# Expert results kept in slot order and gathered back by token half, and rotated sums moved to VectorE

## The chip, the cores and the metric

The kernel runs on one core of a Trainium2 chip. The metric is the device time of one execution in microseconds; of several runs the median stands.

## The reference

The input is x, 4 x 1024 tokens of width 256, float32. One block of the Macaron kind: half a feed-forward layer, attention, half a feed-forward layer, each behind a layer norm. The feed-forward layer sends every token to two of eight experts (width 176).

```python
def _L0_ffn_ref(hidden_states, gate_w, w_gate, w_up, w_down):
    x = hidden_states.reshape(-1, d)
    probs = jax.nn.softmax((x @ gate_w.T).astype(jnp.float32), axis=-1)
    top_w, sel = jax.lax.top_k(probs, TOP_K)                  # TOP_K = 2 of E = 8
    top_w = top_w / jnp.sum(top_w, axis=-1, keepdims=True)
    w_te = jnp.zeros((t, e), logits.dtype).at[jnp.arange(t)[:, None], sel].add(top_w)
    g = jnp.einsum('td,edf->tef', x, w_gate)
    u = jnp.einsum('td,edf->tef', x, w_up)
    out = jnp.einsum('tef,efd->td', silu(g) * u * w_te[:, :, None], w_down)

def _L0_attn_ref(hidden_states, Wq, Wk, Wv, Wo):              # 16 heads of 16
    q, k, v = (proj(Wq), proj(Wk), proj(Wv))
    # _apply_rope: concatenate([x1 * cos - x2 * sin, x2 * cos + x1 * sin])
    q, k = _apply_rope(q, cos, sin), _apply_rope(k, cos, sin)
    probs = softmax(q k^T / 4 + causal)
    return (probs v) Wo^T

x = x + 0.5 * _L0_ffn_ref(_layernorm(x), ...)
x = x + _L0_attn_ref(_layernorm(x), ...)
x = x + 0.5 * _L0_ffn_ref(_layernorm(x), ...)
```

## The kernel before

**Tiles and phases.** The 4096 tokens are 32 token tiles of 128 rows; x_sb holds them in SBUF all the time. Phases run one after the other, with a barrier between: set-up, ffn_phase (f1), projection_phase, attention_phase, output_phase, ffn_phase (f2). Every engine has its own program, written out in order; semaphores connect them. There is no scheduler: what stands first in an engine's program is done first, and an instruction that waits holds up all behind it on its engine.

**Routing in ffn_phase.** Normalised rows go to xn_dram. VectorE picks each token's two experts, and ranks turn into a slot number for each of the 8192 pairs (token, choice). The pairs of one expert lie in a row of slot tiles of 128; with every expert's last tile filled up there are at most SLOT_TILES = 71 of them. Which token stands in which slot is found by one-hot products: VectorE compares slot_p with all rows (at_row, L493) and slot_j with all slot tiles (tile_hits, L475 to L477), in four lots of 16 columns of pairs, and TensorE multiplies the two (64 matmuls over the first 16 slot tiles; 64 of 110 columns over the other 55, L670). `owners` (L483 to L486) makes of the products the row to which each slot's result goes (pair_i) and the token that it reads (token_i). Then comes the list of the experts by tile (L510 to L520), on which TensorE's first expert product waits.

**Expert steps.** For each slot tile j: POOL gathers 128 rows of xn_dram by token_i with an indirect DMA (L378, seventeen steps ahead); TensorE turns it, multiplies by the gate and up weights (L691), turns h (L699) and multiplies by the down weights (L709), each in high and low parts; ScalarE and VectorE do what lies between, ScalarE's last piece being y_copy (L593) into y_sb, eight tiles deep. Two steps later POOL scatters the tile to y_dram by pair_i with a second indirect DMA (L382). So y_dram holds the results by token: both rows of a token side by side. SP has nothing to do in these steps; it waits for the last scatter.

**The end of f2.** SP loads y_dram, 256 KB a token tile (L362), VectorE adds both weighted rows to x_sb (L554), ScalarE issues eight output stores of 512 KB.

**Projection.** f1's results are added here. SP loads y in the same 256 KB pieces (L938, eight deep); ScalarE weighs the first row (L1065), POOL adds it (mix_first, L976), VectorE weighs and adds the second (mix_second, L1038), eight tiles ahead of the projection. VectorE's moments (L112 and those behind it) go into the norm factors, once for four tiles, on POOL (L981, L982). Then for each token tile: ScalarE normalises, TensorE turns and projects q, k and v, VectorE multiplies q and k by cosines and sines (turn_angles: L1023, L1026, L1027), POOL adds the two products (add, L993, roped), TensorE turns the sum, and it is split in three parts by ScalarE, VectorE (rest, L1032), ScalarE and POOL (r_low, L987), and stored by SP. At step t an engine works on tile t, or on t−2 and t−3 where it comes later in this chain.

## Time and profile before

| | us |
|---|---|
| Median of three runs | 1216.24 |
| The runs' span | 1216.02 to 1219.74 |
| The profiled execution | 1216.84 |
| Its span in the trace | 1215.1 |
| Expert steps of f1, 99.36 to 266.68 | 167.32 |
| Projection, 275.39 to 409.34 | 133.95 |
| Expert steps of f2, 1004.75 to 1173.32 | 168.57 |
| Behind f2's last y_copy, 1173.32 to 1215.10 | 41.78 |

Over the span TensorE is busy for 83%, VectorE for 70%, ScalarE for 52% and POOL for 48%; such shares are means over stages with different limits. Stages are read one at a time: the windows say which engine is full in a stage, the chain of waits which engine was last at a place, the timelines when an instruction began, how long it took, and in brackets how long its engine had been idle before it and what ended that. A busy POOL during an indirect DMA is the time in which it makes the transfer's list, not the transfer.

### The profile page before, as it was taken

What the parts mean: (1) busy time and instruction counts of PE and PEld (TensorE: products, weight loads), DVE (VectorE), ACT (ScalarE), POOL (GpSimd) and SP (SyncE); (2) the same over time, 40 slices, a digit from 0 to 9 for tenths busy, and PEclk for the clock granted to TensorE, in tenths of its full rate; (3) what the DMA queues carried; (4) which work ended last, traced back from release to release, by engine and by line L of the source; (5) the groups of instructions that cost most, each with busy time, mean ns of one, the idle gap of its engine ahead of it and who ended that gap; (6) DMA issues with size and microseconds to landing.
All of it is one profiled execution on the core that took longest, in us unless ns stands there. A gap on an engine that the chain in (4) does not pass through costs nothing. (4 is left out here: it accounts for less than half of the span.)

```text
span 1215.1 us, 24056 instructions
## 1 busy us (share of the span) xinstructions
PE 1002.9 (83%) x6998; PEld 644.2 (53%) x6998; DVE 846.8 (70%) x2632; ACT 630.8 (52%) x1318; POOL 588.9 (48%) x756
## 2 busy tenths in 40 slices
PE   1649998974888489999999999999988569998850
PEld 1438997863767223333333333333347349998750
DVE  5585444435999498999989998988529684443347
ACT  1504554444777216666666666666774505554430
POOL 2937777765999302222222222222239127777740
PEclk9857999996999659999999999999989858999985
DMA  6803333325565511111111111110022413333349
GB/s 212 278 12 102 105 102 104 105 92 158 155 180 164 161 61 47 57 56 60 59 57 57 56 60 55 55 54 2 2 75 71 140 31 105 104 103 104 104 149 338
DMA packets 84524, 121.19 MB, mean 100 GB/s; under 512 B 10920, under 2 KB 63920, under 8 KB 81200
## 3 DMA queue, kind: packets, MB, share of 16 engines
q1 hardware_dynamic: 63424, 75.08, 19.8%
q0 software_dynamic: 13632, 37.24, 9.7%
q10 hardware_dynamic: 7344, 7.34, 1.8%
q8 instruction: 63, 1.03, 0.4%
q14 instruction: 61, 0.50, 0.1%
HBM read 75.51 MB, written 43.78 MB: 98 GB/s over the span
## 5 line engine op out<-in xcount | busy, mean ns | idle before, releaser
L1352 ACT ACTIVATE a_probs<-a_ps_s 128x1024 f32<-128x1024 f32 (+3 forms) x384 | 294.2, 813 | 172.8 <-PE a_ps_s L1384 171.6
L1267 POOL TENSOR_SCALAR_AFFINE_SELECT a_probs<-a_probs 128x256 f32<-128x256 f32 x256 | 102.9, 408 | 368.9 <-ACT a_probs L1352 366.2
L1285 DVE CUSTOM_DVE_ANT_0 a_unused<-a_ps_m,const_sb 128x128 bf16<-128x128 f32 (+3 forms) x512 | 234.1, 485 | 26.6 <-PE a_ps_m L1369 16.7
L1369 PE MATMUL a_ps_m<-st_k,st_q 96*128 96x512 bf16 (+3 forms) x768 | 219.6, 344 | 22.3 <-PEq L167 14.9
L378 POOL DMA_INDIRECT v_sb<-xn_dram,f_token_i x142 | 139.7, 984 | 104.7 <-DVE f_token_i L486 62.0
L1287 DVE TENSOR_REDUCE a_max_a<-a_ps_m 128x1 f32<-128x512 f32 x256 | 175.7, 686 | 13.9 <-PE a_ps_m L1369 13.7
L1384 PE MATMUL a_ps_s<-st_q,st_k 98*128 98x512 bf16 (+3 forms) x768 | 180.6, 329 | 1.5 <-ACT a_probs L1352 1.4
L532 DVE TENSOR_TENSOR f_h<-f_ps_gu,f_sg 128x176 f32<-128x176 f32 x142 | 48.5, 341 | 185.2 <-ACT f_sg L598 185.1
L1369 PEld LDWEIGHTS a_ps_m<-st_k,st_q 96*128 96x128 bf16 x768 | 67.8, 98 | 194.3 <-DVE a_max_a L1287 55.2
L1397 PE MATMUL a_ps_ctx<-a_probs,a_v_st 128*32 128x512 f32 (+3 forms) x1536 | 163.6, 498 | 1.3 <-POOL a_probs L1267 0.7
L382 POOL DMA_INDIRECT y_dram<-v_sb,f_pair_i x142 | 140.0, 986 | 44.0 <-issue 38.1
L593 ACT ACTIVATE v_sb<-f_ps_y 128x256 f32<-128x256 f32 x142 | 54.7, 385 | 109.3 <-DMA y_dram<-v_sb,f_pair_i 82.1
L1384 PEld LDWEIGHTS a_ps_s<-st_q,st_k 98*128 98x128 bf16 x768 | 65.3, 98 | 72.3 <-ACT a_probs L1352 42.6
L691 PE MATMUL f_ps_gu<-w_gu_hi,f_xT_hi 128*128 x284 | 96.1, 338 | 9.1 <-DVE f_xT_lo L527 4.2
L691 PE MATMUL f_ps_gu<-w_gu_hi,f_xT_lo 128*128 x284 | 93.2, 328 | 0.0
L691 PE MATMUL f_ps_gu<-w_gu_lo,f_xT_hi 128*128 x284 | 93.0, 327 | 0.0
L709 PE MATMUL f_ps_y<-w_dn_hi,f_hT_hi 88*128 x284 | 92.5, 326 | 0.1
L709 PE MATMUL f_ps_y<-w_dn_lo,f_hT_hi 88*128 x284 | 80.1, 282 | 0.0
L709 PE MATMUL f_ps_y<-w_dn_hi,f_hT_lo 88*128 x284 | 79.4, 280 | 0.0
L588 ACT ACTIVATE f_xT_hi<-f_ps_xT 128x256 fp32r<-128x256 f32 x142 | 54.0, 380 | 46.9 <-PE f_ps_xT L681 46.5
L598 ACT ACTIVATE f_sg<-f_ps_gu 128x176 f32<-128x176 f32 x142 | 44.8, 316 | 53.4 <-PE f_ps_gu L691 53.4
L699 PE MATMUL f_ps_hT<-const_sb,f_h 128*88 128x128 f32 x284 | 55.7, 278 | 10.3 <-DVE f_h L532 9.9
(193 smaller groups left out, 2018.8 us busy)
## 6 DMA issues: line engine op xcount, KB each, us to landing
xn_dram<-v_sb SPq DMA_DIRECT2D x64, 128.0 KB, 3.7
v_sb<-y_dram SPq DMA_DIRECT2D x32, 256.0 KB, 5.5
st_q<-qk_dram SPq DMA_DIRECT2D x16, 384.0 KB
st_k<-qk_dram SPq DMA_DIRECT2D x16, 384.0 KB
st_q<-y_dram SPq DMA_DIRECT2D x16, 256.0 KB, 3.3
st_k<-y_dram SPq DMA_DIRECT2D x16, 256.0 KB, 3.2
qk_dram<-st_rT_hi SPq DMA_DIRECT2D x16, 256.0 KB, 3.0
qk_dram<-st_rT_mid SPq DMA_DIRECT2D x16, 256.0 KB, 3.5
```

The lines of the kernel that those rows point to most:

```text
L378: pool.indirect_dma_start(xg[:, slot, :], None, xn_dram, bass.IndirectOffsetOnAxis(ap=token, axis=0)).then_inc(gathered[slot], 16)
L382: pool.indirect_dma_start(y_dram, bass.IndirectOffsetOnAxis(ap=pair, axis=0), y_sb[:, slot, :], None).then_inc(scattered[slot], 16)
L691: mm = pe.matmul(ps_gu[b][:, 0:2 * F], x_part[:, b, k, :], w_part[:, bass.ds(e, 1), k, :].rearrange("p a f -> p (a f)"), start=(n == 1), s ...
L699: mm = pe.transpose(ps_hT[b][:, c, :], h[:, b, c * FH:(c + 1) * FH], ident)
L709: mm = pe.matmul(ps_y[b], h_part[:, b, c, :], w_part[:, bass.ds(e, 1), c, :].rearrange("p a f -> p (a f)"), start=(n == 1), stop=(n == 6))
L1267: pool.affine_select(out=tri, in_=tri, compare_op=ALU.is_ge, fill=zero, base=0, pattern=[[0, 2], [1, P]], channel_multiplier=-1).then_inc( ...
L1285: dve.tensor_tensor_reduce(unused[:, bank, 0:nk], ps, cst("mask")[:, HALF - nk:HALF], 1.0, NEG, ALU.add, ALU.max, at).then_inc(taken, 1)
L1287: dve.tensor_reduce(at, ps, AX.X, ALU.max).then_inc(taken, 1)
L1352: act.activation(probs[:, s % 4, :, 0:nq], ps_s[s % 2][:, :, 0:nq], ACT.Exp, scale=float(HD) ** -0.5).then_inc(exp_done, 1)
L1369: pe.matmul(ps_m[bank][:, 0:nk], q_st[b][0:MAX_ROW, h, P * i:P * i + P], k_st[b][0:MAX_ROW, h, k0:k0 + nk], start=True, stop=True).then_in ...
L1384: mm = pe.matmul(ps_s[s % 2][:, n, 0:nq], k_st[b][:, h, P * j:P * j + P], q_st[b][:, h, q0:q0 + nq], start=True, stop=True)
L1397: mm = pe.matmul(ps_ctx[32 * h:32 * h + 32, q0 - HALF * half:HALF], v_st[b % 2][:, j, h, :], probs[:, (2 * v + h // 2) % 4, h % 2, 0:nq], ...
```

## The change

**Slots by token half.** The pairs of the first 16 token tiles get the slot tiles 0 to 38, those of the other 16 the tiles 39 to 77: each half with its own list of experts and its own filling, 78 tiles in place of 71. The weights are indexed by tile, as before. The one-hot products run in three passes: slot tiles 0 to 15 and 16 to 38 over the first half's two lots, 39 to 77 over the second half's two, with 32 matmuls each. `owners` no longer makes pair_i.

**Results in slot order.** SP stores each y tile as it stands (plain DMA, 128 KB, L383). The slot number of each pair stays in SBUF as y_rows, and a row group of 128 results is gathered back from y_dram by an indirect DMA on POOL (gather_y). There are 64 such groups, two for each token tile.

**First half's rows.** In both passes its 32 groups are gathered inside the expert loop, one a step from step 43 on, behind one wait for the first 39 stores, and added to x_sb by VectorE from step 46 on. In f2 SP also stores the first four outputs inside the loop.

**Second half's rows.** In f2 POOL waits for all stores and gathers the 32 groups one after the other; VectorE adds them, ScalarE stores. In f1 they are gathered in the projection, five in four steps from step −7 to step 17 (GATHERS), weighed by ScalarE two steps later, and added by POOL another step later; VectorE no longer adds a row there.

**Rotated sums.** `add` (the sum that goes into roped) is issued by VectorE, behind `rest`, in place of POOL.

Cut to its core:

```diff
-SLOT_TILES = TOPK * NT + E - 1
+HALVES = 2
+HT = NT // HALVES
+CT = TOPK * HT + E - 1
+SLOT_TILES = HALVES * CT
+ROWS_OF_HALF = TOPK * HT
 LOT = 16
 LOTS = TOPK * NT // LOT
 DEEP = 8
 XDEEP = 16
+YB = 8
+Y_LAG = 4
+MIX_LAG = 3
...
+def token_row(m):
+
+    return 2 * (m // 4) + m % 2, m // 2 % 2
+
+def rows_mixed(t):
+
+    return 4 * (t // 2) + t % 2 + 3
...
+        LOTS_OF = [range(half, LOTS, HALVES) for half in range(HALVES)]
+        PASSES = [(0, FIRST, LOTS_OF[0]), (FIRST, CT, LOTS_OF[0]), (CT, SLOT_TILES, LOTS_OF[1])]
+        at_tile = [sb(f"at_tile{i}", [P, len(lots), 2 * (j1 - j0), LOT], BF16) for i, (j0, j1, lots) in enumerate(PASSES)]
...
+        OUT_AT = [CT + Y_LAG + MIX_LAG + 8 * (q + 1) - 1 for q in range(HT // 4 - 1)] + [SLOT_TILES - 1]
+
+        def store_out(eng, q):
+
+            eng.wait_ge(mixed, 8 * (q + 1))
+            eng.dma_start(out[q * 4 * P:(q + 1) * 4 * P, :].rearrange("(t p) d -> p t d", p=P), x_sb[:, 4 * q:4 * q + 4, :]).then_inc(out_stored, 16)
...
+            for j in range(SLOT_TILES):
+                sp.wait_ge(y_out, j + 1)
+                sp.dma_start(y_dram[j * P:(j + 1) * P, :], y_sb[:, j % DEEP, :]).then_inc(stored[j % DEEP], 16)
+                if out is not None and j in OUT_AT:
+                    store_out(sp, OUT_AT.index(j))
             for q in range(DEEP):
-                sp.wait_ge(scattered[q], 16 * len(range(q, SLOT_TILES, DEEP)))
+                sp.wait_ge(stored[q], 16 * len(range(q, SLOT_TILES, DEEP)))
             if out is not None:
-                for t in range(NT):
-                    sp.wait_ge(mixed, t - 7 + 8)
-                    sp.dma_start(yb[:, t % 8, :, :].rearrange("p c d -> p (c d)"),
-                                 y_dram[t * P * TOPK:(t + 1) * P * TOPK, :].rearrange("(p c) d -> p (c d)", c=TOPK)
-                                 ).then_inc(y_in[t % 8], 16)
                 sp.wait_ge(out_stored, 16 * (NT // 4))
...
-            def scatter(j, slot, pair):
-                pool.wait_ge(y_out, j + 1)
-                pool.indirect_dma_start(y_dram, bass.IndirectOffsetOnAxis(ap=pair, axis=0), y_sb[:, slot, :], None).then_inc(scattered[slot], 16)
-
-            def step(j, u, token, pair):
-
-                if token is not None:
-                    if j + XDEEP + 1 == FIRST:
-                        pool.wait_ge(slots_ready, 2)
+            def gather_y(m):
+                t, c = token_row(m)
+                wait(pool, mixed, m - YB + 1)
+                row = y_rows[:, c * NT + t:c * NT + t + 1]
+                pool.indirect_dma_start(yg[:, m % YB, :], None, y_dram[0:CT * P, :] if m < ROWS_OF_HALF else y_dram, bass.IndirectOffsetOnAxis(ap=row, axis=0)).then_inc(y_in[m % YB], 16)
+
+            def wait_stored(tiles):
+                for q in range(DEEP):
+                    pool.wait_ge(stored[q], 16 * len(range(q, tiles, DEEP)))
+
+            for j in range(-XDEEP - 1, SLOT_TILES + 2):
+                ahead = j + XDEEP + 1
+                if is_tile(ahead):
+                    if ahead in (FIRST, CT):
+                        pool.wait_ge(slots_ready, 2 if ahead == FIRST else 3)
                     wait(pool, xT_ready, j + 2)
-                    gather((j + XDEEP + 1) % XDEEP, token)
-                if pair is not None:
-                    scatter(j - 2, (j - 2) % DEEP, pair)
-
-            def fixed_step(j):
-                step(j, j % 4, token_i[:, j + XDEEP + 1:j + XDEEP + 2] if is_tile(j + XDEEP + 1) else None, pair_i[:, j - 2:j - 1] if is_tile(j - 2) else None)
-
-            for j in range(-XDEEP - 1, SLOT_TILES + 2):
-                fixed_step(j)
+                    gather(ahead % XDEEP, token_i[:, ahead:ahead + 1])
+                if j == CT + Y_LAG:
+                    wait_stored(CT)
+                if 0 <= j - CT - Y_LAG < ROWS_OF_HALF:
+                    gather_y(j - CT - Y_LAG)
+            if out is not None:
+                wait_stored(SLOT_TILES)
+                for m in range(ROWS_OF_HALF, TOPK * NT):
+                    gather_y(m)
...
+            def mix(m):
+                t, c = token_row(m)
+                dve.wait_ge(y_in[m % YB], 16 * (m // YB + 1))
+                if c:
+                    dve.wait_ge(mixed, m - 1)
+                dve.scalar_tensor_tensor(x_sb[:, t, :], yg[:, m % YB, :], w_mix[:, c, t:t + 1], x_sb[:, t, :], ALU.mult, ALU.add).then_inc(mixed, 1)
...
+                if 0 <= j - CT - Y_LAG - MIX_LAG < ROWS_OF_HALF:
+                    mix(j - CT - Y_LAG - MIX_LAG)
...
-            for i in range(TOPK * NT):
-                lot = i // LOT
-                pe.wait_ge(first_hot_ready, lot + 1)
-                mm = pe.matmul(ps_first, at_row[:, lot, :, i % LOT], at_first[:, lot, :, i % LOT], start=(i == 0), stop=(i == TOPK * NT - 1))
-            mm.then_inc(first_owned, 1)
-            for i in range(TOPK * NT):
-                lot = i // LOT
-                pe.wait_ge(later_hot_ready, lot + 1)
-                mm = pe.matmul(ps_later, at_row[:, lot, :, i % LOT], at_later[:, lot % 2, :, i % LOT], start=(i == 0), stop=(i == TOPK * NT - 1))
-                if i % LOT == LOT - 1:
-                    mm.then_inc(later_hot_used if i < TOPK * NT - 1 else later_owned, 1)
+            pe.matmul(ps_before, before_bf[:], hot_sum[:], start=True, stop=True)
+            pe.matmul(ps_total, ones_bf[:, 0:P], hot_sum[:], start=True, stop=True).then_inc(ranks_ready, 1)
+
+            done = 0
+            for i, (j0, j1, lots) in enumerate(PASSES):
+                for n, lot in enumerate(lots):
+                    done = done + 1
+                    pe.wait_ge(one_hot_ready, done)
+                    for k in range(LOT):
+                        mm = pe.matmul(ps_owner[i], at_row[:, lot, :, k], at_tile[i][:, n, :, k],
+                                       start=(n == 0 and k == 0), stop=(n == len(lots) - 1 and k == LOT - 1))
+                mm.then_inc(owned, 1)
...
+GATHERS = {t: [n for n in range(ROWS_OF_HALF) if 4 * n // 5 - 7 == t] for t in range(-20, NT + 20)}
...
+            def gather_y(n):
+                t, c = later_row(n)
+                wait(pool, mixed, n - YB + 1)
+                row = y_rows[:, c * NT + t:c * NT + t + 1]
+                pool.indirect_dma_start(yb(n), None, y_dram, bass.IndirectOffsetOnAxis(ap=row, axis=0)).then_inc(y_in[n % YB], 16)
+
+            def mix(n):
+                t, c = later_row(n)
+                pool.wait_ge(weighted, n + 1)
+                if c:
+                    pool.wait_ge(mixed, n - 1)
+                pool.tensor_tensor(x_sb[:, t, :], yb(n), x_sb[:, t, :], ALU.add).then_inc(mixed, 1)
...
-                if is_tile(t + AHEAD + 1):
-                    mix_first(t + AHEAD + 1)
-                if is_tile(t):
-                    add(t, u % 2)
+                for n in GATHERS[t]:
+                    gather_y(n)
+                for n in GATHERS[t - 3]:
+                    mix(n)
...
+            def add(t, b):
+                dve.wait_ge(angled, 3 * t + 3)
+                wait(dve, rT_ready, t - 1)
+                dve.tensor_tensor(roped[:, b, :].rearrange("p (a j h) -> p a h j", j=HD, h=HG),
+                                  by_cos[:, b, :].rearrange("p (a h j) -> p a h j", j=HD, h=HG),
+                                  by_sin[:, b, :].rearrange("p (a h j) -> p a h j", j=HD, h=HG), ALU.add).then_inc(roped_ready, 1)
...
-            def mix_second(t):
-                dve.wait_ge(begun, t + 1)
-                dve.scalar_tensor_tensor(x_sb[:, t, :], yb(t)[:, 1, :], w_mix[:, 1, t:t + 1], x_sb[:, t, :],
-                                         ALU.mult, ALU.add).then_inc(mixed, 1)
 
             def step(t, u):
                 if t >= 0 and is_tile(t + 1):
                     x_low(t + 1, (u + 1) % 2)
                 if is_tile(t):
                     turn_angles(t, u % 2)
-                if is_tile(t + AHEAD):
-                    mix_second(t + AHEAD)
                 if is_tile(t - 2):
                     rest(t - 2, t - 2)
+                if is_tile(t):
+                    add(t, u % 2)
                 if is_tile(t + AHEAD - 1):
-                    dve.wait_ge(mixed, t + AHEAD)
+                    if t + AHEAD - 1 >= HT:
+                        dve.wait_ge(mixed, rows_mixed(t + AHEAD - 1 - HT))
                     moments_of.tile(t + AHEAD - 1, (t + AHEAD - 1) % 8)
...
+                for n in GATHERS[t - 2]:
+                    weigh(n)
```

POOL from the last expert steps of f1 into the projection, before (the tile named v_sb holds the gathered x and y_sb, st_q and st_k hold y in the projection):

```order
L378 DMA v_sb<-xn_dram,f_token_i 128x256
L382 DMA y_dram<-v_sb,f_pair_i 17280x256 x20
L211 UNCONDITIONAL_BRANCH
L166 ISA x2
L968 UNCONDITIONAL_BRANCH
L971 MEMSET p_minus_half 128x4
L844 MEMSET st_one 32x128
L976 TENSOR_TENSOR x_sb<-st_q,x_sb 128x256 x4
L976 TENSOR_TENSOR x_sb<-st_k,x_sb 128x256 x2
L981 TENSOR_TENSOR rstd<-rstd,p_minus_half 128x4
L982 TENSOR_TENSOR nmr<-nmr,rstd 128x4
```

The same place after:

```order
L402 DMA v_sb<-xn_dram,f_token_i 128x256
L408 DMA v_sb<-y_dram,y_rows 128x256 x15
L227 UNCONDITIONAL_BRANCH
L182 ISA x2
L1001 UNCONDITIONAL_BRANCH
L1004 MEMSET p_minus_half 128x4
L881 MEMSET st_one 32x128
L1011 DMA st_q<-y_dram,y_rows 128x256 x5
L1018 TENSOR_TENSOR x_sb<-st_q,x_sb 128x256 x2
L1023 TENSOR_TENSOR rstd<-rstd,p_minus_half 128x4
L1024 TENSOR_TENSOR nmr<-nmr,rstd 128x4
```

The loop's last POOL work is gathers of y in place of scatters (ahead of these rows they take turns with the gathers of x, one and one, as the scatters did from step 2 on), and in the projection five gathers and two additions stand ahead of the first norm factors, where six additions stood. f2 ends with 47 of L408 in a row.

POOL in the projection, before, from one set of norm factors on:

```order
L981 TENSOR_TENSOR rstd<-rstd,p_minus_half 128x4
L982 TENSOR_TENSOR nmr<-nmr,rstd 128x4
L976 TENSOR_TENSOR x_sb<-st_k,x_sb 128x256
L993 TENSOR_TENSOR p_roped<-p_by_cos,p_by_sin 128x8x4x16
L987 TENSOR_TENSOR st_rT_lo<-p_rT_rest,st_rT_mid 128x4x128
```

The same place after:

```order
L1023 TENSOR_TENSOR rstd<-rstd,p_minus_half 128x4
L1024 TENSOR_TENSOR nmr<-nmr,rstd 128x4
L1011 DMA st_q<-y_dram,y_rows 128x256 x2
L1018 TENSOR_TENSOR x_sb<-st_q,x_sb 128x256
L1029 TENSOR_TENSOR st_rT_lo<-p_rT_rest,st_rT_mid 128x4x128
```

The sum L993 has left POOL, and two gathers have come (one in each of the next three steps).

VectorE in one tile of the projection, before:

```order
L1014 TENSOR_TENSOR p_xT_lo<-p_ps_xT,p_xT_hi 128x256
L1023 TENSOR_TENSOR p_by_cos<-p_ps_qk,const_sb 128x512
L1026 TENSOR_TENSOR p_by_sin<-p_ps_qk,const_sb 128x32x8
L1027 TENSOR_TENSOR p_by_sin<-p_ps_qk,const_sb 128x32x8
L1038 SCALAR_TENSOR_TENSOR x_sb<-st_k,w_mix,x_sb 128x256
L1032 TENSOR_TENSOR p_rT_rest<-p_ps_rT,st_rT_hi 128x512
L112 BN_STATS p_stats<-x_sb 128x6
```

The same tile after:

```order
L1048 TENSOR_TENSOR p_xT_lo<-p_ps_xT,p_xT_hi 128x256
L1056 TENSOR_TENSOR p_by_cos<-p_ps_qk,const_sb 128x512
L1059 TENSOR_TENSOR p_by_sin<-p_ps_qk,const_sb 128x32x8
L1060 TENSOR_TENSOR p_by_sin<-p_ps_qk,const_sb 128x32x8
L1072 TENSOR_TENSOR p_rT_rest<-p_ps_rT,st_rT_hi 128x512
L1065 TENSOR_TENSOR p_roped<-p_by_cos,p_by_sin 128x8x4x16
L128 BN_STATS p_stats<-x_sb 128x6
```

The second mix L1038 has gone, and the rotated sum stands behind the residual.

## Rows read from the trace of the kernel before

**Rows 1.** Windows by stage: stretch, length, busy PE, PEld, DVE, ACT, POOL, clock, DMA.

```profile
99.36:266.68 167.32, 158.45 (x1132) 149.55 (x1132) 72.85 (x212) 86.51 (x283) 127.40 (x132) 0.98 0.33 104
275.39:409.34 133.95, 98.72 (x576) 82.88 (x576) 112.67 (x272) 86.52 (x192) 114.34 (x114) 0.89 0.58 169
1004.75:1173.32 168.57, 158.52 (x1132) 149.32 (x1132) 72.81 (x212) 86.12 (x283) 127.90 (x132) 0.98 0.33 104
1173.32:1215.10 41.78, 0.00 (x0) 0.00 (x0) 27.19 (x64) 0.00 (x0) 1.24 (x2) 0.51 0.86 308
```

**Rows 2.** The chain that ended last, second expert stage: start, us, what.

```profile
1012.17 0.95 PE f_ps_gu L691 x6
...
1073.93 1.10 PE f_ps_gu L691 x6
1075.58 0.97 POOL v_sb L378
...
1078.15 0.97 POOL v_sb L378
...
1173.89 2.42 DMA y_dram<-v_sb,f_pair_i
```

**Rows 3.** Timeline of VectorE, routing of the first pass: start, us, what.

```profile
74.66 1.22 DVE L493 TENSOR_TENSOR v_sb<-f_count_lot,f_slot_p 128x2048 bf16<-128x2048 bf16 x1
...
76.64 1.22 DVE L493 TENSOR_TENSOR v_sb<-f_count_lot,f_slot_p 128x2048 bf16<-128x2048 bf16 x1
...
82.59 0.61 DVE L475 TENSOR_TENSOR f_at_later<-f_count_lot,f_slot_j 128x880 bf16<-128x880 bf16 x1
...
84.25 0.17 DVE L483 SCALAR_TENSOR_TENSOR f_empty<-f_ps_hT,const_sb 128x16 f32<-128x16 f32 x1
...
92.90 0.74 DVE L510 TENSOR_TENSOR f_work<-const_sb,f_first_tile 128x568 f32<-128x568 f32 x1
...
96.37 0.17 DVE L520 CAST f_packed<-f_packed_f 128x10 int32<-128x10 f32 x1
```

**Rows 4.** Timeline of TensorE, the long one-hot product of the first pass.

```profile
84.39 13.39 PE L670 MATMUL f_ps_y<-f_at_later,v_sb 128*128 128x110 bf16 x64 [0.43 <-DVE f_at_later L477]
```

**Rows 5.** Timeline of POOL: gathers of the first pass, first factors of the projection.

```profile
92.97 1.49 POOL L378 DMA_INDIRECT v_sb<-xn_dram,f_token_i  x1 [0.30 <-issue]
...
103.53 0.94 POOL L378 DMA_INDIRECT v_sb<-xn_dram,f_token_i  x1 [0.31 <-issue]
...
285.93 1.22 POOL L981 TENSOR_TENSOR rstd<-rstd,p_minus_half 128x4 f32<-128x4 f32 x1 [1.38 <-DVE nmr L123]
```

**Rows 6.** Windows of the projection, columns as in group 1: four tiles, then three.

```profile
354.82:369.44 14.62, 12.31 (x72) 10.06 (x72) 13.88 (x36) 9.20 (x22) 14.28 (x15) 1.00 0.52 150
388.35:396.62 8.27, 8.27 (x56) 7.48 (x55) 7.00 (x17) 6.31 (x15) 7.32 (x8) 1.00 0.55 164
```

**Rows 7.** Groups by line and shape: xcount, busy us, mean ns, idle before.

```profile
L993 POOL TENSOR_TENSOR p_roped<-p_by_cos,p_by_sin 128x512 f32<-128x512 f32 x32 | 46.0, 1437 | 9.2 <-DVE p_by_sin L1027 8.8
...
L987 POOL TENSOR_TENSOR st_rT_lo<-p_rT_rest,st_rT_mid 128x512 bf16<-128x512 f32 x32 | 37.2, 1163 | 2.4 <-ACT st_rT_mid L1090 2.3
...
L1023 DVE TENSOR_TENSOR p_by_cos<-p_ps_qk,const_sb 128x512 f32<-128x512 f32 x32 | 21.7, 678 | 5.1 <-PE p_ps_v L1129 4.6 <-POOL p_roped L993 0.5
...
L1038 DVE SCALAR_TENSOR_TENSOR x_sb<-st_k,w_mix,x_sb 128x256 f32<-128x256 f32 x16 | 12.1, 759 | 1.6 <-POOL x_sb L976 1.6
L976 POOL TENSOR_TENSOR x_sb<-st_q,x_sb 128x256 f32<-128x256 f32 x16 | 12.1, 763 | 4.1 <-ACT st_q L1065 4.1
...
L981 POOL TENSOR_TENSOR rstd<-rstd,p_minus_half 128x4 f32<-128x4 f32 x8 | 8.3, 1044 | 2.6 <-DVE nmr L123 2.6
...
L438 DVE TENSOR_TENSOR f_hot<-const_sb,f_chosen 128x256 f32<-128x256 f32 x4 | 2.4, 590 | 0.1
```

**Rows 8.** Timeline of VectorE, the last mixes of the kernel.

```profile
1207.25 3.10 DVE L554 SCALAR_TENSOR_TENSOR x_sb<-v_sb,w_mix,x_sb 128x256 f32<-128x256 f32 x7 [0.18 <-DMA v_sb<-y_dram]
```

**Rows 9.** The page's DMA issues: count, KB each, median us to landing.

```profile
xn_dram<-v_sb SPq DMA_DIRECT2D x64, 128.0 KB, 3.7
```

More of the change, by code:

```diff
@@ L440, in _ @@
             dve.wait_ge(lg_ready, NT // 4)
             choose(0, ps_lg)
-            own.then_wait(dve.scalar_tensor_tensor(others[:], hot[:, 0, :, :].rearrange("p e t -> p t e"), NEG, ps_lg, ALU.mult, ALU.add))
+            for half in range(HALVES):
+                of = slice(HT * half, HT * (half + 1))
+                own.inc(dve.scalar_tensor_tensor(others[:, of, :], hot[:, 0, half, :, :].rearrange("p e t -> p t e"), NEG, ps_lg[:, of, :],
+                                                 ALU.mult, ALU.add))
@@ L500, in _ @@
+            for lot in LOTS_OF[0]:
+                row_hits(lot)
+                tile_hits(0, lot)
+            for lot in LOTS_OF[0]:
+                tile_hits(1, lot)
+            owners(0)
+            for lot in LOTS_OF[1]:
+                row_hits(lot)
+                tile_hits(2, lot)
             dve.wait_ge(egap_ready, 1)
@@ L619, in _ @@
             if out is not None:
[L620 to L623 removed]
+                for q in range(HT // 4, NT // 4):
+                    store_out(act, q)
         @block.tensor
@@ L960, in step @@
                     load_stacks((t - 14) // 2)
-            for t in range(YB - 2):
-                load_y(t)
             tiles(sp, step)
```

238 lines of the change are left out of this document (103 added, 135 removed).

## The prediction

> **What bounds the kernel now.** I read the times and the page, then the windows by stage, then the chain that ended last and the timelines where stages meet. The profiled execution took 1216.84 us (span 1215.1), 0.60 above the median of 1216.24, so the sum is made against 1216.84 and 0.60 comes off at the end. In both expert stages TensorE is busy for 158 of some 168 us at a clock of 0.98 [rows 1]. POOL is at 127: each step it issues a gather and a scatter, two indirect DMAs, and in the chain they stand 2.57 us apart (1075.58 to 1078.15) where the products of an expert step go on every 2.13 us (1012.17 to 1073.93, 29 tiles) [rows 2]. So POOL falls behind, and the chain runs through it in the stage's second part. In the projection VectorE and POOL are both nearly full: of a stretch of four tiles, 14.62 us, they are busy for 13.88 and 14.28; late, when no y is left to mix, a tile takes 2.76 us (8.27 over three) and TensorE is full, VectorE busy 7.00 [rows 6]. After the last product of the second pass nothing runs on TensorE for 41.78 us: y comes back and is mixed there [rows 1].
>
> **Routing, twice.** From the first one-hot operation (74.66) to the first expert product (99.36) are 24.70 us [rows 1, 3]. TensorE's second one-hot product sets the end: 64 matmuls of 110 columns, 13.39 us, 0.21 each [rows 4], and VectorE is through with its list at 96.54 [rows 3]. Now 96 matmuls run in place of 128, none wider than 78 columns, over half the lots each. VectorE's work: two lots of 16 tiles as before, 1.98 each (74.66 to 76.64); two lots of 23 tiles, below the 1.66 that a lot of 55 takes (82.59 to 84.25), I take 1.1; owners, three operations of some 0.2, twice 0.6; two lots of 39 tiles with their rows, 1.22 for the rows and below 1.66 for the tiles, I take 2.6; the weights of the mix 0.9 (estimate: four operations of 0.17 to 0.35 with gaps); the expert list as before, 3.64 (92.90 to 96.54) [rows 3]. Together 4.0 + 2.2 + 1.2 + 5.2 + 0.9 + 3.6 = 17.1. TensorE's last 16 matmuls start when the last lot is there, at 12, and end by 12 + 16 x 0.21 = 15.4, before the list: the bound has gone over to VectorE. With owners of the third pass and the first x_low behind the list, as now, the first product stands at about 18.9, **5.7 us earlier** in each pass (4 if the 23- and 39-tile lots cost as much as 55; 7 if they shrink with the size).
>
> **Expert steps, twice.** 78 slot tiles in place of 71. From the first product to that of tile 3 it is 7.4 (1004.75 to 1012.17) [rows 1, 2], then 74 steps at 2.135 (2.13, and a little for weights that change), 158.0, and 4.7 from the last gate and up product to the last y_copy (two steps and a copy, an estimate): 170.1. Before it was 167.32 and 168.57 [rows 1], since 71 such steps would have needed only 155 and POOL's pairs cost the rest. So seven more tiles cost **+2.8 and +1.5**, not 15. y now leaves by SP, which has nothing else to do there; a store lands in 3.7 us or less [rows 9], and y_sb is eight deep.
>
> **Gathers of y in the loop.** From step 43 to 60 POOL again issues two indirect DMAs a step (x and y), 2.57 against 2.13: it drifts 18 x 0.44 = 7.8 us. x is gathered 15 tiles ahead, so that takes no harm; a row of y has three steps, 6.4 us, less the landing (2.42 for a scatter [rows 2]), so some 4 us of drift are free. Of the remaining 3.8 VectorE's slack takes part (busy 72.85 of 167, with 32 mixes of 0.44 to come [rows 1, 8]). I take **+1.5** a pass, 0 and 7.8 being the ends. The wait for 39 stored tiles at step 43 stands on POOL ahead of the x gathers; it should be met: y 38 is copied at about step 40, 3.7 us is under two steps.
>
> **Projection.** At its start, before, 256 KB loads, weighing and two additions a tile came ahead of the first factors. Now the first 16 token tiles are mixed already, but five gathers (0.94 and 0.31 of issue, 1.25 apart [rows 5]) and two additions (0.76 [rows 7]) stand on POOL ahead of the first factors: 7.8 us and a wait for the first landing, 8.1, where it was 10.5 (275.39 to 285.93 [rows 1, 5]): −2.4. VectorE loses the second mix (0.76) and gains the rotated sum. Its price is not in the trace: as one two-input operation on 512 elements it lies between 0.68 (the same size out of PSUM) and 1.18 (two of 256 elements with both inputs in SBUF, 0.59 each); POOL took 1.44 [rows 7]. Both inputs lie in SBUF and the output is strided, so I take 1.0: +0.24 a tile. POOL must do, before VectorE can turn to tile 21 (now at 369.44, where the four-tile stretch ends [rows 6]; counted back from the last tile): 32 gathers x 1.25, 30 additions x 0.76, 17 residuals x 1.16 and 6 factors x 1.04 [rows 5, 7], together 89; from 275.39 that ends at 364.5, 5 us ahead of VectorE today, so POOL is no bound if nothing stretches. But beside VectorE a gather took 1.49 in place of 0.94 [rows 5]; one in four stretched costs 4.3 and brings POOL nearly level. VectorE: −2.4 + 21 x 0.24 = +2.6. I take +3 at tile 21; +1 for tiles 21 to 24. Late, VectorE's 2.33 a tile becomes 3.3 over TensorE's 2.76, +0.5 for seven tiles: +3.5. The last sum is off POOL, −0.5. Together **+7** (−3 at 0.68 and no wait; +16 if all 32 gathers stretch by 0.54).
>
> The Trainium skill (page "SBUF — State Buffer", section "Door 1") says that SBUF has 16-byte cachelines and that each access to a new line pays a penalty. The sum writes with a step of 16 bytes. By that it would stand at the upper end, 1.18, and the projection at about +12; no row here shows it on VectorE.
>
> **The tail of the second pass.** Before: 41.78 [rows 1]. After: the last store lands (3.7 [rows 9]), then POOL issues 32 gathers 1.25 apart, 40.0 [rows 5], which nothing can hide, for every second-half row may lie in the last tiles; then a landing of some 2 (2.42 for a scatter), one mix of 0.44 (3.10 over seven, [rows 8]) and the output store as before, 4.75 (1210.35 to the end of the stage at 1215.10 [rows 1, 8]): 50.9, so **+9.1**. That the first half is mixed under the experts gains little, since 32 issues cost as much as 32 loads of twice the size did.
>
> **Sum.** First pass −5.7 + 2.8 + 1.5 = −1.4; projection +7; second pass −5.7 + 1.5 + 1.5 + 9.1 = +6.4; in all +12.0 on 1216.84, less 0.60: 1228.2, rounded to **1228 us**. Attention and output projection are untouched.
>
> **Rivals.**
> Gathers pace everything (slower still). If a gather stretches to 1.49 + 0.30 whenever VectorE reads two operands from SBUF, half of the tail's and half of the projection's cost +8.6 each (16 x 0.54; 4.3 of it is in the forecast), and both loops pay their drift in full, +6.3 each: 1228 + 8.6 + 4.3 + 12.6 = 1253.5. For it: the 1.49 beside VectorE's 92.90 operation [rows 3, 5]. Against: the next gathers at 0.94, and that expert operations of VectorE read PSUM. The point from which it decides is a drift over 4 us.
> The Trainium skill (the same page, section "Who interferes with whom") says that a VectorE instruction with two SBUF inputs contends with GpSimd's reads, and takes that descriptor generation needs the write side; by that the mixes would leave the gathers alone, and this rival would lose its cause. The 1.49 above speaks against.
>
> Cover holds (no change). The sum costs 0.68, no row of y is late: passes −2.9 and +4.9, projection −1.5 (−2.4 at the start, nothing for 21 tiles, +0.2 a late tile, less the end): +0.5, 1216.7.
>
> Projection pays (faster). VectorE and POOL each wait for the other's two-input operations now; with the sum off POOL, at 0.68, and the mix off VectorE, POOL's gathers need no operands, and four tiles take 13.9 in place of 14.62 over the first 21: −2.4 − 3.8 − 0.8: −7. With both loops free: −2.9 + 4.9 − 7 = −5.0, 1211. It decides where the sum stays under the mix's 0.76 and POOL never is waited for. Against: POOL is at 14.28 of 14.62 today and gets 1.25 gathers a tile.
>
> **How the numbers follow.** Forecast 0.60 (1220 to 1241: ends of routing ±1.5 a pass, loops −1.5 to +3, projection ±5, summed as independent); no change 0.15; faster 0.11; gathers pace 0.14. A difference under 0.3%, 3.6 us, can't be told from none. Faster by more: most of that rival and little of the no-change case, 0.11; within: 0.15; slower: 0.74. The range 1212 to 1246 leaves out half of the fast rival's and two thirds of the gather rival's chance and the forecast's own ends.
>
> **What would show it.** First expert product 18 to 20 us after the first one-hot operation, with VectorE last; expert stages of 169 to 173 us with no POOL in the chain to step 43; in the projection the rotated sum at 1.0, gathers at 0.94 to 1.1 and tile 21 three us later in the stage; late tiles of 3.3; a tail of 51 us whose chain is 32 gathers. Wrong would it be if the tail's gathers go at another pace than 1.25, if the sum is far from 1.0, or if the factors at the projection's start wait for the gathers' rows.

## The result and the profile after

The changed kernel takes 1239.43 us (median of four runs, 1238.99 to 1240.88) against 1216.77 for the kernel before: 1.0184 times as long, 95% interval 1.0164 to 1.0203. The forecast was 1228, slower; the range to 1246 holds the time, the size was 11 us short. The profiled execution took 1240.88 us, its span 1238.9; against the span of before (1215.1) that is +23.8, and this difference is taken apart here.

The windows by stage of the changed kernel (columns as in rows 1: first the expert steps of f1, then the projection, the expert steps of f2, and what follows f2's last y_copy):

```profile
93.64:263.59 169.95, 168.67 (x1244) 163.87 (x1244) 92.80 (x265) 98.64 (x311) 97.66 (x103) 0.99 0.50 140
267.34:424.00 156.66, 105.59 (x576) 87.07 (x576) 127.05 (x272) 87.15 (x192) 108.17 (x114) 0.88 0.41 117
1018.01:1188.40 170.39, 169.37 (x1244) 164.22 (x1244) 93.11 (x265) 99.22 (x311) 96.72 (x102) 0.99 0.53 149
1188.40:1238.90 50.50, 0.00 (x0) 0.00 (x0) 15.38 (x32) 0.00 (x1) 30.26 (x32) 0.52 0.46 140
```

Beside [rows 1]: TensorE is now busy in 99% of the expert steps (before 94 to 95%), the projection has grown from some 134 to some 157 us, and POOL, busy for 1.24 us of the tail before, has 32 issues there. In the table the second number of a forecast for expert steps is the term for the gathers of y in the loop. The whole by terms (us; negative is a gain):

| Term | Before | After | Measured | Forecast |
|---|---|---|---|---|
| First one-hot operation to first expert product, f1 | 24.70 | 18.48 | −6.2 | −5.7 |
| Expert steps, f1 | 167.32 | 169.95 | +2.6 | +2.8 +1.5 |
| Last y_copy of f1 to the projection's start | 8.71 | 3.75 | −5.0 | 0 |
| Projection's start to the first turned tile | 19.52 | 19.13 | −0.4 | −2.4 |
| Tile 0 to tile 21 | 74.53 | 96.74 | +22.2 | +5.4 |
| Tile 21 to tile 31 | 29.73 | 33.82 | +4.1 | +4.5 |
| First one-hot operation to first product, f2 | 24.68 | 18.51 | −6.2 | −5.7 |
| Expert steps, f2 | 168.57 | 170.39 | +1.8 | +1.5 +1.5 |
| Behind f2's last y_copy | 41.78 | 50.50 | +8.7 | +9.1 |

The rest (+0.5 ahead of f1's one-hot operations, +1.6 from tile 31 to f2's) makes up the 23.8. One term is far off, the first 21 tiles of the projection, and one gain had not been seen, the hand-over from f1.

Timeline of VectorE and TensorE, routing of f1 (start, us, what):

```profile
75.16 1.22 DVE L515 TENSOR_TENSOR v_sb<-f_count_lot,f_slot_p 128x2048 bf16<-128x2048 bf16 x1
...
91.56 0.17 DVE L567 CAST f_packed<-f_packed_f 128x11 int32<-128x11 f32 x1
...
93.64 0.66 PE L729 MATMUL f_ps_gu<-w_gu_hi,f_xT_hi 128*128 x1 [0.73 <-DVE f_xT_lo L573]
```

Where before TensorE's long one-hot product [rows 4] ended last, now VectorE's list does: it is written at 91.73, 16.6 us after the first operation (forecast 17.1), and the first product follows.

The projection: windows of four tiles (from tile 5's turn to tile 9's), and of three late ones:

```profile
307.56:325.44 17.88, 12.37 (x72) 10.08 (x72) 16.94 (x35) 11.20 (x25) 16.61 (x17) 1.00 0.38 107
404.40:414.21 9.81, 8.90 (x53) 7.35 (x52) 9.81 (x19) 6.49 (x15) 3.51 (x3) 1.00 0.68 197
```

Beside [rows 6] four tiles take 17.88 in place of 14.62. VectorE is busy for 16.94, and POOL for 16.61; five issues of 0.15 to 0.30 that don't count as busy make POOL's share some 17.5. Both are nearly full again. Late tiles take 3.27 and VectorE has no gap, as forecast (3.3). The groups by shape of this stage (xcount, busy, mean ns, idle before):

```profile
L1065 DVE TENSOR_TENSOR p_roped<-p_by_cos,p_by_sin 128x512 f32<-128x512 f32 x32 | 42.6, 1333 | 0.1
L1029 POOL TENSOR_TENSOR st_rT_lo<-p_rT_rest,st_rT_mid 128x512 bf16<-128x512 f32 x32 | 37.5, 1175 | 28.1 <-ACT st_rT_mid L1126 28.1
L1011 POOL DMA_INDIRECT st_q<-y_dram,y_rows x32 | 32.3, 1008 | 6.6 <-issue 5.7 <-POOL x_sb L1018 0.6
L1018 POOL TENSOR_TENSOR x_sb<-st_q,x_sb 128x256 f32<-128x256 f32 x32 | 29.6, 933 | 0.5
```

The rotated sum costs 1.33 us, not 1.0, and POOL's additions 0.93, not 0.76 as in [rows 7]: each blocks the other. A pair that shows it:

```profile
313.81 1.47 DVE L1065 TENSOR_TENSOR p_roped<-p_by_cos,p_by_sin 128x512 f32<-128x512 f32 x1
...
314.24 1.50 POOL L1018 TENSOR_TENSOR x_sb<-st_q,x_sb 128x256 f32<-128x256 f32 x1
```

Of POOL's 28.1 us of waits for ScalarE's middle part 20.5 lie behind tile 21, where it has no gathers left. From the first turned tile to tile 21 (286.47 to 383.21) it waited for this:

```profile
POOL rstd L1023 <- DVE nmr L139: 10.6, 6, 3.7
POOL st_rT_lo L1029 <- ACT st_rT_mid L1126: 7.6, 5, 3.9
```

So POOL's program goes in step with the tiles: it stands still for 18.2 us there, with the gathers of later steps behind it in its program. What ScalarE itself waited for:

```profile
ACT st_q L1101 <- DMA st_q<-y_dram,y_rows: 27.0, 17, 7.3
ACT p_xn L1106 <- POOL nmr L1024: 12.5, 8, 2.6
```

Seventeen times the row to be weighed had not landed, and the weighing stands ahead of the tile's normalisation. The longest stall between two tiles, 9.99 us from tile 14's turn to tile 15's (timeline of SP, ScalarE and VectorE):

```profile
344.67 0.84 SPq L911 DMA_DIRECT2D st_q<-qk_dram  x1
...
354.14 0.51 ACT L1101 ACTIVATE st_q<-st_q,w_mix 128x256 f32<-128x256 f32 x1 [5.14 <-DMA st_q<-y_dram,y_rows]
...
357.10 0.42 DVE L1048 TENSOR_TENSOR p_xT_lo<-p_ps_xT,p_xT_hi 128x256 fp32r<-128x256 f32 x1 [5.79 <-ACT p_xT_hi L1111]
```

The first load of the attention's stacks goes out at 344.67 beside three stores, and POOL issues a gather at 344.67 and another at 346.00. The rows of these two are weighed at 354.14 and 355.80, so a landing took up to 9.8 us here; that the load caused it was not tested. ScalarE idles 5.14 us for a row until 354.14, and VectorE 5.79 us behind ScalarE.

The tail of f2 in the chain that ended last (start, us, what):

```profile
1188.43 1.74 DMA y_dram<-v_sb
...
1191.19 0.94 POOL v_sb L408
...
1229.94 2.69 DMA v_sb<-y_dram,y_rows
```

A store of y lands, then 32 gathers follow 1.25 apart from 1191.19 to 1229.94, then the last landing: the tail is POOL's issues, as worked out. Three times the chain passes through a landing (2.95 to 3.90 us) in place of issues, but the issues stay 1.25 apart there too.

### The profile page after: what moved, and what is told of

Read it like the earlier page. It is cut to its first block and busy times, and to the rows that moved or that the text cites. A ratio compares the mean times of both kernels' runs of the same rounds, so it can differ in the third digit from the quotient of the medians.

```text
span 1238.9 us, 24878 instructions
## 1 busy us (share of the span) xinstructions
PE 1015.7 (82%) x7158; PEld 667.6 (54%) x7158; DVE 884.6 (71%) x2696; ACT 657.0 (53%) x1374; POOL 545.6 (44%) x724
## 5 line engine op out<-in xcount | busy, mean ns | idle before, releaser
L402 POOL DMA_INDIRECT v_sb<-xn_dram,f_token_i x156 | 150.1, 962 | 155.8 <-PE f_ps_xT L719 74.3
L408 POOL DMA_INDIRECT v_sb<-y_dram,y_rows x96 | 92.2, 960 | 47.1 <-issue 42.8
L729 PE MATMUL f_ps_gu<-w_gu_hi,f_xT_hi 128*128 x312 | 105.3, 337 | 2.2 <-DVE f_xT_lo L573 1.4
L729 PE MATMUL f_ps_gu<-w_gu_lo,f_xT_hi 128*128 x312 | 102.0, 327 | 0.0
L729 PE MATMUL f_ps_gu<-w_gu_hi,f_xT_lo 128*128 x312 | 101.8, 326 | 0.0
L747 PE MATMUL f_ps_y<-w_dn_hi,f_hT_hi 88*128 x312 | 100.9, 323 | 0.1
L747 PE MATMUL f_ps_y<-w_dn_lo,f_hT_hi 88*128 x312 | 87.6, 281 | 0.0
L747 PE MATMUL f_ps_y<-w_dn_hi,f_hT_lo 88*128 x312 | 87.4, 280 | 0.0
L635 ACT ACTIVATE v_sb<-f_ps_y 128x256 f32<-128x256 f32 x156 | 60.0, 385 | 44.5 <-PE f_ps_y L747 43.9
L590 DVE SCALAR_TENSOR_TENSOR x_sb<-v_sb,w_mix,x_sb 128x256 f32<-128x256 f32 x96 | 45.8, 478 | 43.3 <-DMA v_sb<-y_dram,y_rows 43.3
```

The lines of the kernel that those rows point to most:

```text
L402: pool.indirect_dma_start(xg[:, slot, :], None, xn_dram, bass.IndirectOffsetOnAxis(ap=token, axis=0)).then_inc(gathered[slot], 16)
L408: pool.indirect_dma_start(yg[:, m % YB, :], None, y_dram[0:CT * P, :] if m < ROWS_OF_HALF else y_dram, bass.IndirectOffsetOnAxis(ap=row, a ...
L635: act.activation(y_sb[:, u, :], ps_y[u % 2], ACT.Copy).then_inc(y_out, 1)
L729: mm = pe.matmul(ps_gu[b][:, 0:2 * F], x_part[:, b, k, :], w_part[:, bass.ds(e, 1), k, :].rearrange("p a f -> p (a f)"), start=(n == 1), s ...
L747: mm = pe.matmul(ps_y[b], h_part[:, b, c, :], w_part[:, bass.ds(e, 1), c, :].rearrange("p a f -> p (a f)"), start=(n == 1), stop=(n == 6))
```

## Experiments

The first theory (V) was that VectorE bounds the projection and the sum there is dear; the rival (G) that POOL's gathers and their landings pace it. All times are medians; the ratios go against runs of the kernel before on the same chip (1217.4 to 1218.3). The changed kernel itself stands against 1216.77, so a difference taken from its 1239.43 is uncertain by some 1.5 us.

**1. The sum written in a row.**

```diff
-    dve.tensor_tensor(roped[:, b, :].rearrange("p (a j h) -> p a h j", j=HD, h=HG),
+    dve.tensor_tensor(roped[:, b, :].rearrange("p (a h j) -> p a h j", j=HD, h=HG),
```

> The changed kernel, but VectorE's rotated sum writes its 512 numbers in the order in which it reads them, not with a step of 16 bytes; the heads' columns of q and k then stand in another order (the only thing that is left out of the reference). Theory V (VectorE bounds the projection, and the sum there is dear): if the strided write is what makes it dear, the sum falls from 1.33 us to some 0.7 to 0.9 and the time by 32 x 0.4 to 0.6, to 1221 to 1227. If the stride costs nothing, the sum stays at 1.09 alone and 1.45 beside POOL, and the time at 1239. Theory G (POOL's gathers and their landings pace the projection): 1236 to 1239 whatever the sum costs.

Measured 1236.0 (1.0142, 1.0123 to 1.0160). The sum's line in the changed kernel (xcount, duration ns min/median/max):

```profile
L1065 DVE TENSOR_TENSOR p_roped<-p_by_cos,p_by_sin x32: 1065/1274/2086, 287.9 to 418.9; 128x512 f32<-128x512 f32 x32
```

The same line in this kernel:

```profile
L1065 DVE TENSOR_TENSOR p_roped<-p_by_cos,p_by_sin x32: 676/978/1686, 288.0 to 413.2; 128x512 f32<-128x512 f32 x32
```

The stride costs 0.39 us a sum on VectorE (1.065 to 0.676 where nothing else interferes), over 32 sums some 12 us of VectorE; the time fell by 3.4. So VectorE's work alone isn't the pace. The Trainium skill's rule (page "SBUF — State Buffer", section "Door 1") has each access to a new 16-byte line pay a penalty; on VectorE the trace agrees, at 0.39 us for this sum, and run 11 below looks at POOL.

**2. Plain loads in place of the projection's gathers.**

```diff
-    pool.indirect_dma_start(yb(n), None, y_dram, bass.IndirectOffsetOnAxis(ap=row, axis=0))
+    sp.dma_start(yb(n), y_dram[(CT + n) * P:(CT + n + 1) * P, :])     # in SP's step t, for n in GATHERS[t]
```

> The changed kernel, but in the projection SP loads the 32 row groups with plain 128 KB transfers (so rows of other tokens are added); POOL issues no gather there. Theory V: the sum and VectorE stay as they are, only the waits for landings go (5.8 us at tile 15, some 2 at tile 3), and four tiles still take about 17: 1230 to 1234. Theory G: the projection falls back to 3.4 to 3.6 us a tile, 1217 to 1222.

Measured 1216.26 (0.9986, 0.9975 to 0.9996): 23 us less than the changed kernel. Theory V as it stood falls. Window of four tiles:

```profile
298.02:313.35 15.33, 12.13 (x72) 10.09 (x72) 15.26 (x35) 11.17 (x27) 10.77 (x12) 1.00 0.52 146
```

Without gathers VectorE is full (15.26 of 15.33), POOL idle for nearly a third. Tiles 0 to 21 take 79.2 us, +4.7 against before, about what the forecast had for the whole effect there (+5.4), and the first tile turns 12.4 us after the stage's start in place of 19.1. The gathers are worth the rest: 6.7 at the start and 17.5 up to tile 21. The time lies just under the span of G.

**3. Weighing later.**

```diff
-    for n in GATHERS[t - 2]: weigh(n)        # ScalarE
-    for n in GATHERS[t - 3]: mix(n)          # POOL
+    for n in GATHERS[t - 4]: weigh(n)
+    for n in GATHERS[t - 5]: mix(n)
```

> The changed kernel, but a gathered row group is weighed by ScalarE four steps after its issue, not two, and added by POOL five steps after, not three. Theory V: the wait for landings at tiles 3 and 15 goes, nothing else: 1231 to 1235. Theory G: landings cost more than those two places, 1220 to 1230. If landings cost nothing: 1239.

Measured 1231.45 (1.0100, 1.0083 to 1.0116), 8.0 less. The first tile turns 14.6 us after the start, tiles 0 to 21 take 90.9, and the stall at tile 15 is gone. By the number alone this is V's outcome, just above G's span; with run 2, the landings are one part and the gathers have another. Four tiles still take as long as before this edit (tiles 9 to 13 here; tiles 5 to 9 took 17.86 at a granted clock of 1.00, so the 0.90 of this window is not the reason):

```profile
318.46:336.36 17.90, 13.43 (x72) 11.44 (x72) 16.50 (x35) 11.14 (x25) 16.62 (x17) 0.90 0.45 125
```

So landings cost some 10 us of the stage (4.6 at the start, 5.8 up to tile 21), and 11.7 are left between this kernel and the second over the first 21 tiles.

**4. The sum ahead of the residual on VectorE.**

```diff
     turn_angles(t, u % 2)
+    add(t, u % 2)
     rest(t - 2, t - 2)
-    add(t, u % 2)
```

> The changed kernel, but VectorE does the rotated sum right behind the three products, ahead of the residual of the tile two before. Theory V with contention: the sum then stands beside POOL's gathers and additions in place of POOL's residual; its mean goes from 1.33 to 1.1 to 1.2 and the time to 1233 to 1237. Without contention, or by theory G: 1238 to 1240.

Measured 1240.54 (1.0174, 1.0144 to 1.0204): nothing gained. Tiles 0 to 21 take 93.8, 2.9 less, and tiles 21 to 31 37.1, 3.3 more. The sum's mean is 1.39, the gathers' 1.11 (1.01 in the changed kernel), the additions' 0.81: the blocking went from one pair to another. Eight of the 32 gathers take 1.50 to 1.62, each beside a sum (two do in the changed kernel); others beside a sum stay at 0.96 to 1.03, so what decides it stays open.

**5. Thin additions.** The theory now (P): POOL itself is full with gathers, stretched additions and residuals; the rival (C): the gathers slow VectorE.

```diff
-    pool.tensor_tensor(x_sb[:, t, :], yb(n), x_sb[:, t, :], ALU.add)
+    pool.tensor_tensor(x_sb[:, t, 0:8], yb(n)[:, 0:8], x_sb[:, t, 0:8], ALU.add)     # on the kernel of 3
```

> As e3 (late weighing), and POOL adds only 8 of the 256 columns of a gathered row group; the other columns are left out of x. 32 gathers stay. Theory P (since e2: POOL is full with its gathers, its stretched additions and its residuals, 17.7 of the 17.9 us of four tiles): without the additions POOL has some 14 and VectorE sets the pace, as in e2, 15.3 us for four tiles: 1217 to 1222. Theory C (the gathers slow VectorE itself): four tiles stay at 17 or more and the time at 1228 to 1232.

Measured 1220.72 (1.0030, 1.0019 to 1.0042):

```profile
315.66:331.70 16.04, 12.12 (x72) 10.10 (x72) 15.64 (x36) 11.12 (x26) 12.59 (x17) 1.00 0.49 140
```

With 32 gathers in place but the additions cut, POOL has room (12.59) and VectorE sets the pace (15.64 of 16.04), 0.7 above the second kernel. P holds: 9.8 of the 11.7 us go with POOL's load. A thin addition also blocks VectorE less, whose busy time falls from 16.50 to 15.64, so this run alone doesn't part POOL's load from the blocking; but run 2 keeps the full additions (mean 0.97) and run 5 the gathers, and either way VectorE is back as the pace. Some 2 us over 21 tiles stay with the gathers, and their cause was not separated further.

**6. The sum alone moved, in the kernel before.**

```diff
-    add(t, u % 2)     # POOL's step, waits for the products
+    add(t, u % 2)     # VectorE's step, behind rest
```

> The kernel before with one part of the change alone: VectorE does the rotated sum, behind the residual. Theory V: VectorE keeps the second mix there, 13.9 us of four tiles, and gets four sums of 1.1 to 1.3 more: 18 to 19.5 us in place of 14.6 for the first 24 tiles, 3.3 for the last seven: 1238 to 1248. Theory P (POOL is what counts): POOL loses 5.7 us of four tiles: 1210 to 1217.

Measured 1236.7 (1.0160, 1.0143 to 1.0177), a little under the span of V:

```profile
315.28:332.72 17.44, 12.09 (x72) 10.09 (x72) 17.37 (x39) 10.74 (x24) 9.48 (x11) 1.00 0.56 157
```

VectorE alone is full. Moving the sum costs 2.9 us for four tiles there, and only taking the second mix off VectorE, which needs POOL for the additions, pays most of it back (2).

**7. The sum back on POOL.**

```diff
-    add(t, u % 2)     # VectorE's step
+    add(t, u % 2)     # POOL's step, behind the additions
```

> The changed kernel with the rotated sum given back to POOL, all else as changed. Theory P: POOL, full already, gets four sums of 1.44 to 1.5 more for four tiles, 21 to 23 us in place of 17.9, for some 20 tiles, and gives back 0.5 for each of the last eleven: 1250 to 1262. Theory V: VectorE loses 1.33 a tile and the projection falls below the 1239 of the changed kernel.

Measured 1243.33 (1.0214, 1.0196 to 1.0232), below the forecast span:

```profile
308.77:329.11 20.34, 13.79 (x72) 11.25 (x72) 14.08 (x31) 11.44 (x26) 19.13 (x21) 0.88 0.39 110
```

POOL is full, 2.5 us more for four tiles than in the changed kernel; I had expected 3 to 5. Tiles 21 to 31 give back 3.7 (30.1 in place of 33.8), but then ScalarE waits 5.6 us for stores of heads (0.4 in the changed kernel), and the last of them is issued 3.6 later in the stage. With gathers on POOL the sum is dear on either engine.

**8. Late sums on POOL.**

```diff
-    if is_tile(t): add(dve, t, u % 2)
+    if is_tile(t) and t < 22: add(dve, t, u % 2)      # on the kernel of 3
+    if is_tile(t) and t >= 22: add(pool, t, u % 2)    # POOL's step
```

> As e3, and POOL does the rotated sum for the tiles from 22 on, where it has no gathers left. All of the computation is kept. By the rows of before and after a late tile takes 2.76 with the sum on POOL and 3.2 to 3.3 with it on VectorE: ten tiles by 0.5 less: 1225 to 1228, below e3 (1231) and still above the kernel before.

Measured 1231.44 (1.0109, 1.0083 to 1.0136), no better than 3. Tiles 21 to 31 take 31.3 in place of 34.5, but tiles 0 to 21 take 1.5 more, and the stage ends no sooner:

```profile
410.67 0.60 ACT L1127 ACTIVATE st_rT_hi<-p_ps_rT 128x512 bf16<-128x512 f32 x1 [3.53 <-DMA qk_dram<-st_rT_lo]
```

Towards the end ScalarE waits 5.7 us in two waits for a store of heads to land before it splits the next (none in run 3), and the last store is issued 154.1 us after the stage's start, in run 3 after 152.5. The gain of 5 that I expected was not there.

**9. One more gather at the end of f1.**

```diff
+    pool.wait_ge(y_out, SLOT_TILES)
+    gather(0, token_i[:, 0:1])
```

> The changed kernel with one more gather of x by POOL at the very end of the first pass, behind the last y_copy; SP waits for it too. It asks where the 5.0 us went by which the change shortened the stretch from the first pass's last y_copy to the projection's start (8.71 to 3.74). Theory H1 (the end of a phase takes longer when POOL has just issued an indirect DMA): the stretch grows to 7.5 to 9, the time to 1243 to 1245. Theory H2 (it was only the queue of scatters that POOL had left to issue, and the landing of the last): the stretch grows by the gather's own issue and landing, 3.74 to some 5 to 5.5, the time by 1 to 2.

Measured 1248.58 (1.0255, 1.0236 to 1.0274), 9 us more. POOL's timeline about the end of f1, first in the kernel before:

```profile
267.76 0.97 POOL L382 DMA_INDIRECT y_dram<-v_sb,f_pair_i  x1 [0.30 <-issue]
275.39 0.10 POOL L971 MEMSET p_minus_half<- 128x4 f32 x1 [6.66 <-POOLq L167]
```

Then in the changed kernel:

```profile
267.34 0.10 POOL L1004 MEMSET p_minus_half<- 128x4 f32 x1 [18.62 <-POOLq L183]
```

And in this one:

```profile
264.07 0.94 POOL L404 DMA_INDIRECT v_sb<-xn_dram,f_token_i  x1 [15.21 <-ACT v_sb L640]
...
275.81 0.10 POOL L1009 MEMSET p_minus_half<- 128x4 f32 x1 [10.80 <-POOLq L183]
```

One gather of 0.94 us puts the next phase off by 8.5: POOL idles for 10.80 behind it. The stretch from the last y_copy (263.80) to the next phase is 12.0: H2 falls, and H1 holds in kind, with its sizes too small (7.5 to 9, and 1243 to 1245). The changed kernel's last indirect DMA of f1 is 18.62 us old when the next phase begins, and its wait is hidden under the last expert steps.

**10. Half of the tail's gathers as plain loads.**

```diff
-    for m in range(ROWS_OF_HALF, TOPK * NT): gather_y(m)
+    for m in range(ROWS_OF_HALF, TOPK * NT, 2): gather_y(m)
+    # SP, for every other m: sp.dma_start(yg[:, m % YB, :], y_dram[(m + 7) * P:(m + 8) * P, :])
```

> The changed kernel, but in the tail of the second pass every second row group is loaded by SP with a plain 128 KB transfer (rows of other tokens are added there). Theory I (the tail is POOL's issues, 32 by 1.25): 16 issues less, the tail falls from 50.5 by 16 to 20 us to 30 to 35 and the time to 1219 to 1223. Theory D (the transfers or the mixes behind them set the tail): it falls by less than 8, 1232 or more.

Measured 1221.56 (1.0034, 1.0016 to 1.0053). The tail, with the columns of rows 1:

```profile
1185.98:1218.20 32.22, 0.00 (x0) 0.00 (x0) 13.83 (x32) 0.01 (x1) 15.40 (x16) 0.55 0.69 219
```

18.3 us less for 16 issues less (16 x 1.25 would be 20.0): theory I.

**11 and 12. Ordered weights.** The columns of Wq and Wk are put into the turned heads' order in the set-up, so that the sum needs no stride; 11 on the kernel before, 12 on the kernel of 3.

```diff
-    pool.tensor_tensor(roped[:, b, :].rearrange("p (a j h) -> p a h j", j=HD, h=HG), ..., ALU.add)
+    pool.tensor_tensor(roped[:, b, :], by_cos[:, b, :], by_sin[:, b, :], ALU.add)      # 11; dve in 12
```

> The kernel before with the columns of Wq and Wk put into the order of the turned heads once, in the set-up, so that POOL's rotated sum reads and writes 512 numbers in a row and VectorE's products do so too; all of the computation is kept. From e1: without the stride VectorE's sum fell from 1.07 to 0.68 at its shortest. If POOL pays for the stride as well, its sum falls from 1.44 towards the 1.16 of its residual, four tiles lose up to 1.1 us of POOL, and VectorE (13.9 of 14.6) is the next bound: 1212 to 1216. If POOL doesn't pay for the stride: 1216 to 1219.

> As e3 (late weighing), with the columns ordered as in e11, so that VectorE's rotated sum writes in a row; all of the computation is kept. Theory P: POOL stays full; its additions are blocked for a shorter time by the sum: four tiles 16.9 in place of 17.9, as e1 showed, and late tiles 3.0 in place of 3.3: 1223 to 1228. If VectorE had set the pace: 1217 to 1221.

Measured 1220.01 (1.0021, 1.0005 to 1.0036) and 1226.08 (1.0062, 1.0049 to 1.0075). POOL's sum in 11:

```profile
L993 POOL TENSOR_TENSOR p_roped<-p_by_cos,p_by_sin 128x512 f32<-128x512 f32 x32 | 45.4, 1420 | 9.4 <-DVE p_by_sin L1025 9.4
```

POOL pays nothing for the stride (1.42, before 1.44 in [rows 7]), so 11 gains nothing, and lies above its span by 1. In 12 four tiles take as long as in 1, POOL still the fuller one with its issues counted; the time is within the span of P:

```profile
318.73:335.75 17.02, 12.10 (x72) 10.09 (x72) 15.24 (x35) 11.14 (x25) 15.77 (x17) 1.00 0.47 132
```

12 is the best version of the change that computes all of it, 13 us faster than the change as it was made, and still 0.6% slower than the kernel before. No kernel here that computes all of it beats the one before.

## Why the prediction was right, and where it fell short

- **Routing** (−5.7 a pass): right, −6.2 in each pass. The bound went from TensorE's product to VectorE's list, as said; the 23- and 39-tile lots took 1.0 and 2.5 us with their parts (taken at 1.1 and 2.6).
- **Expert steps** (+2.8, +1.5): right at +2.6, +1.8. TensorE is busy for 99%.
- **Gathers of y in the loop** (+1.5 a pass): nothing is left for this term. The drift was there (from 187.83 to 190.33 a pair of gathers took 2.50 us, against 2.13 for a step), and the mixes' slack held it. (18 x 0.44 is 7.9 and not 7.8, which changes nothing.)
- **Hand-over** (0): wrong by 5.0 to the good; the prediction has no term for it. The 6.66 us of POOL's idle time behind the last scatter stood in the trace of before, and run 9 shows that such a wait belongs to an indirect DMA shortly before the end of a phase.
- **Projection, start** (−2.4): −0.4. The first factors came 8.0 us after the stage's start, as worked out (8.1), but ScalarE weighs a row ahead of normalising and waited for landings; run 3 gets 4.6 us back there.
- **Projection, tiles 0 to 21** (+5.4): this step failed; it measured +22.2. The failing sentence is that POOL "ends at 364.5, 5 us ahead of VectorE today, so POOL is no bound if nothing stretches". It added up POOL's whole work from the stage's start, as if POOL could do it ahead. The total was not far off: from the stage's start to tile 21 POOL is busy for 90.0 us, with some 6 more between issues. But its program stands in step with the tiles, and the other 19 of the 115.9 us are waits; so the count for four tiles is what matters: 5 x 1.25 + 5 x 0.76 + 4 x 1.16 + 1.04 = 15.7 by the prediction's own rows, over 14.62 already, and with the prices of the changed trace (gathers 1.01 and some 0.25 of issue, additions 0.93, residuals 1.18, factors 1.04 and 0.20) 16.9; in the window of 17.88 it was 17.5, since three of its five additions there took some 1.5. Run 5 shows the cause: take POOL's load away and the 17.9 become 16.0. The second part is the landing. The prediction puts one at 2 to 2.4 us; beside the first stack load one took up to 9.8, and ScalarE's order handed the delay to every engine (5.8 us, run 3). The 22.2 are then 5.8 of landings (run 3), 9.8 of POOL's load (run 5), 2.0 of gathers not explained, and 4.7 of VectorE's own (run 2).
- **The sum's price** (1.0): 1.33; alone 1.07, of which 0.39 is the stride (1). VectorE's own share of the loss, without gathers, came out near the forecast (run 2: +4.7 to tile 21, +4.1 late). Up to tile 21 that is luck: at the 1.27 that the sum costs in run 2 the forecast's own way of counting gives 21 x 0.51 = 10.7, but VectorE had 0.74 us free in four tiles before [rows 6], which the forecast did not count.
- **Late tiles** (+4.5): +4.1, at the 3.3 us a tile named.
- **Tail** (+9.1): +8.7, 32 issues of 1.25. The 3.7 of a store's landing is a median and no bound, as the prediction reads it (up to 5.1 in the trace of before); the last store of y landed in 1.74.
- **Rivals.** "Gathers pace everything" had the right actor in the wrong places: loops and tail went on at a median of 0.95 (single gathers up to 1.23), and in the projection it is not the stretch of the gather but its room in POOL's step and its landing. Cover did not hold, and "projection pays" fell with its condition, a sum under 0.76. Even with loads in place of gathers (run 2) the projection doesn't pay: its first tile turns 7.1 us earlier in the stage than before the change, and 4.7 and 4.1 are lost behind it.

The range was held since its upper end took in a mechanism beside the one that came; the forecast's own span (to 1241) just reached the time. That is luck as well: without the 5.0 of the hand-over, for which it has no term, the time would have been some 1244.
